# Attention stacks kept by feature in DRAM and read in 4 KB pieces, with another order of work where the second layer begins

## The reference, cut to what matters

```
def rope(t):                       # t1, t2: the two halves of a head's 32 features
    return concat([t1 * cos - t2 * sin, t2 * cos + t1 * sin])
def attn(q, k, v):
    return softmax(q k^T / sqrt(32)) v, heads side by side
xn = adaln(x, cond, ln1);  q, k, v = xn @ qkv_w.T;        x = x + attn(rope(q), rope(k), v) @ sa_out_w.T
xn = adaln(x, cond, ln2);  q = xn @ q_w.T;  k, v = ctx @ k_w.T, ctx @ v_w.T
                                                          x = x + attn(rope(q), rope(k), v) @ ca_out_w.T
xn = adaln(x, cond, ln3);                                 x = x + gelu(xn @ ffn_w1.T + b1) @ ffn_w2.T + b2
```

## Time and profile before

| | |
|---|---|
| median of 3 runs | 1928.59 us (1923.56 to 1931.18) |
| the profiled execution | 1925.28 us, span 1923.5 us |
| mean granted clock of TensorE | 0.994 |
| packets, all queues | 306451, 308.37 MB |
| attention stage | to about 1240 us |

### The profile page before, as it was taken

One profiled execution on the slowest core, in us unless ns is written; L12 is line 12 of the kernel. 1 busy time (PEld: TensorE's weight loads), 2 busy tenths in 40 slices (PEclk: granted clock), 3 DMA queues, 4 the chain that ended last, 5 costly groups with the idle time before them and its releaser, 6 DMA issues. The chain is left out here.

```text
span 1923.5 us, 39339 instructions
## 1 busy us (share of the span) xinstructions
PE 1869.4 (97%) x13460; PEld 1630.4 (85%) x13460; DVE 1294.9 (67%) x2250; ACT 1383.3 (72%) x3813; POOL 785.8 (41%) x818
## 2 busy tenths in 40 slices
PE   8899999999998999999999998899999999999999
PEld 7788888888877888888888886688898998989898
DVE  7766676767776677676776776446667666666754
ACT  4777777888876888888888888655666666565654
POOL 3534433443442454454454441013536354444531
PEclk9999999999998999999999999999999999999999
DMA  7666676566576778767668677343232322323130
GB/s 232 195 203 185 204 223 194 177 200 198 165 220 189 204 212 233 201 197 227 199 200 225 198 217 190 109 137 110 78 99 67 99 88 89 95 71 110 45 99 33
DMA packets 306451, 308.37 MB, mean 160 GB/s; under 512 B 21072, under 2 KB 260048, under 8 KB 306256
## 3 DMA queue, kind: packets, MB, share of 16 engines
q1 hardware_dynamic: 304528, 304.47, 53.4%
q10 hardware_dynamic: 1728, 1.39, 0.3%
HBM read 212.46 MB, written 92.27 MB: 158 GB/s over the span
## 5 line engine op out<-in xcount | busy, mean ns | idle before, releaser
L744 ACT ACTIVATE ps_s<-ps_s,neg_max 128x256 f32<-128x256 f32 x1024 | 452.8, 443 | 55.4 <-DVE neg_max L861 48.3
L861 DVE TENSOR_REDUCE neg_max<-ps_s 128x2 f32<-128x512 f32 x512 | 349.3, 687 | 212.8 <-PE ps_s L615 212.4
L758 ACT ACTIVATE prob<-ps_s 128x512 f32<-128x512 f32 x512 | 303.4, 593 | 137.2 <-PE ps_s L634 134.3
L634 PE MATMUL ps_s<-qT,kT 98*128 98x256 f32 x1024 | 211.6, 289 | 24.4 <-DMA qT<-max_rows 21.8
L931 POOL TENSOR_TENSOR rope_c<-rope_c,rope_s 128x256 f32<-128x256 f32 x128 | 98.4, 769 | 330.5 <-DVE rope_s L836 330.5
L615 PE MATMUL ps_s<-kT,qT 96*128 96x256 f32 x1024 | 216.5, 293 | 10.7 <-ACT ps_s L744 8.3
L615 PEld LDWEIGHTS ps_s<-kT,qT 96*128 96x128 f32 x1024 | 169.9, 190 | 60.3 <-ACT ps_s L744 28.4
L605 PE MATMUL ps_g<-xx_hi,w_hi 128*128 128x256 f32 x1024 | 208.1, 285 | 1.4 <-issue 1.4
L634 PEld LDWEIGHTS ps_s<-qT,kT 98*128 98x128 f32 x1024 | 169.3, 191 | 46.9 <-issue 21.0
L744 ACT ACTIVATION_READ_ACCUMULATOR ps_s<-ps_s,neg_max 128x1 f32 x1024 | 207.8, 203 | 0.0
L605 PE MATMUL ps_g<-xx_lo,w_hi 128*128 128x256 f32 x1024 | 205.5, 282 | 0.0
(11 more groups left out here) (155 smaller groups left out, 4654.7 us busy)
## 6 DMA issues: line engine op xcount, KB each, us to landing
kT<-k_turned SPq DMA_DIRECT2D x384, 128.0 KB, 3.1
qT<-q_turned SPq DMA_DIRECT2D x128, 256.0 KB, 3.9
f_raw<-in_w1T SPq DMA_DIRECT2D x124, 256.0 KB, 3.1
k_turned<-rot_hi SPq DMA_DIRECT2D x64, 256.0 KB, 3.2
k_turned<-rot_lo SPq DMA_DIRECT2D x64, 256.0 KB, 2.5
q_turned<-rot_hi SPq DMA_DIRECT2D x64, 256.0 KB, 3.6
q_turned<-rot_lo SPq DMA_DIRECT2D x64, 256.0 KB, 4.1
qT<-q_turned SPq DMA_DIRECT2D x128, 128.0 KB, 3.9
```

Of the source, the lines that this page charges most:

```text
L634: ins = eng.matmul(ps_s[:, score_bank(step), t * L:(t + 1) * L], kT[:, quad % NQ, j, t * P:(t + 1) * P], qT[:, quad % NQ, j, :], start=Tru ...
L744: ins = eng.activation(scores[:, t * L:(t + 1) * L], scores[:, t * L:(t + 1) * L], ACT.Exp, bias=neg_max[G % 2][:, t, j:j + 1], accum_out= ...
L758: eng.activation(prob[:, n % NP, :, :].rearrange("p t l -> p (t l)"), ps_s[:, score_bank(step), :], ACT.Exp).then_inc(exp_done, 1)
L861: eng.tensor_reduce(neg_max[G % 2][:, :, j], ps_s[:, score_bank(step), :].rearrange("p (t l) -> p t l", l=L), AX.X, ALU.max, negate=True). ...
```

## The change

`turned[m]` gets the shape (2, 2, HD, H, L): item parity, part, feature of a head, head, token, so that one feature of four neighbouring heads is one piece of 4 KB. A spill is made in four copies instead of two (per part and half of the heads' features). A stack is read with two copies for k and two for q: q's rows are high, low, high and k's high, high, low in blocks of 32, and k's two blocks of high come in one copy whose source is repeated. In `stage_order` the places around items 14 to 17 are changed: the projections k, q, v of item 16 and the output projections of item 13 follow each other without a gap, the second layer's weight rows for k, q and v are loaded from place 632 to 707 and split from 668 to 723, and item 17's norm, context and projections come up to six places later.

```diff
--- before.py
+++ after.py
@@ -90,20 +90,20 @@
                 put(p + place, kind, n, h)
         if ahead < N + 2:
 
-            late = 0
+            late = 6 if ahead == B + 1 else 0
             steps = {2: (2, 4, 5, 8, 10), B + 1: (-3, 0, 1, 5, 8), N: (-14, -12, -11, -6, -4),
                      N + 1: (-26, -24, -23, -18, -16)}.get(ahead, (-13, -5, -4, 1, 5))
             for place, step in zip(steps, (("stats", ahead, 0), ("stats", ahead, 1), ("norm", ahead), ("scale", ahead, 0), ("scale", ahead, 1))):
                 put(p + late + place, *step)
-            x_place = p + late + (31 if ahead == B else {N: 6, N + 1: -10}.get(ahead, 22 if ahead == 2 else 18 if B < ahead else 16))
+            x_place = p + late + (29 if ahead == B else {N: 6, N + 1: -10}.get(ahead, 22 if ahead == 2 else 18 if B < ahead else 16))
             for half in range(2):
                 put(x_place + 3 * half, "turn_x", ahead, half)
                 put(x_place + 2 + 3 * half, "x_high", ahead, half)
                 put(x_place + 4 + 3 * half, "x_low", ahead, half)
         if ahead < N:
             if ahead >= B:
-                put(p - 10, "ctx_load", ahead)
-                put(p + 9, "ctx_split", ahead)
+                put(p + (-6 if ahead <= B + 1 else -10), "ctx_load", ahead)
+                put(p + (14 if ahead == B + 1 else 9), "ctx_split", ahead)
             k, q, v = (project(m, ahead, 0) + project(m, ahead, 1) for m in "kqv")
             if ahead in (1, 2):
                 begins = {1: (48, 65, 79), 2: (40, 51, 66)}[ahead]
@@ -119,15 +119,20 @@
                 turns(spread(p + 35, 18, q))
                 spread(p + 68, 16, v)
             else:
-                turns(spread(p + 18, 11, k))
-                spread(*((p + 42, 9, v) if ahead == B else (p + 42, 13, v)))
-            if 2 < ahead < N - 1:
-                turns(spread(*((p + 42, 13, q) if ahead < B else (p + 50, 10, q) if ahead == B else (p + 29, 13, q))))
+                for m, units in zip("kqv", (k, q, v)):
+                    place, count = {B: {"k": (29, 11), "q": (40, 11), "v": (51, 10)},
+                                    B + 1: {"k": (24, 10), "q": (34, 11), "v": (45, 10)}}.get(
+                                        ahead, {"k": (18, 11), "q": (29, 13), "v": (42, 13)})[m]
+                    last = spread(p + place, count, units)
+                    if m != "v":
+                        turns(last)
+            if 2 < ahead < B:
+                turns(spread(p + 42, 13, q))
         if i >= 1:
             put(p + 37, "res_load", i - 1)
 
-            spread(p + (3 if i == N - 1 else 7) + 48, 14 if i >= N - 2 else 9, [("project", "o", i - 1, t, c) for cs in (range(KC - 1), (KC - 1,)) for t in range(T) for c in cs])
-            put(p + 66, "store", i - 1)
+            spread(p + {B - 2: 61, N - 1: 51}.get(i, 55), 14 if i >= N - 2 else 10 if i in (B - 2, B - 1) else 9, [("project", "o", i - 1, t, c) for cs in (range(KC - 1), (KC - 1,)) for t in range(T) for c in cs])
+            put(p + (72 if i == B - 2 else 66), "store", i - 1)
         if i == N - 1:
             put(p + 68, "res_load", i)
             for c in range(KC - 1):
@@ -140,9 +145,11 @@
             weight_rows(44, layer_rows(0, "o"), 4, 8)
             put(60, "b1_load")
         if i == B - 2:
-            weight_rows(p + 6, layer_rows(1, "k"), 3, 8)
-            weight_rows(p + 19, layer_rows(1, "q"), 3, 8)
-            weight_rows(p + 28, layer_rows(1, "v"), 3, 8)
+            for n, m in enumerate("kqv"):
+                for c, row in enumerate(layer_rows(1, m)):
+                    put(p + (-40, 3, 20)[n] + (7, 5, 5)[n] * c, "w_load", *row)
+                    put(p + (-4, 14, 31)[n] + (4, 5, 5)[n] * c, "w_high", *row)
+                    put(p + (-4, 14, 31)[n] + (4, 5, 5)[n] * c + LOW, "w_low", *row)
         if i == B:
             weight_rows(p + 66, layer_rows(1, "o"), 3, 8)
         if i == N - 2:
@@ -325,7 +332,7 @@
     with ExitStack() as whole:
 
 
-        turned = {m: nc.dram_tensor(f"{m}_turned", (2, D, 2, L), F32, kind="Internal").ap() for m in "qk"}
+        turned = {m: nc.dram_tensor(f"{m}_turned", (2, 2, HD, H, L), F32, kind="Internal").ap() for m in "qk"}
 
         def sem(name):
             return whole.enter_context(nc.semaphore(name))
@@ -420,7 +427,7 @@
             stack_in = {m: [sem(f"stack_{m}{n}") for n in range(4)] for m in "qk"}
             max_rows_in = [sem(f"max_rows_in{n}") for n in range(2)]
 
-            STACKS = {"q": 2, "k": 3}
+            STACKS = {"q": 2, "k": 2}
 
             mod_done, mod_turned, x_turned, product_done, scores_done, max_turned, weigh_done, mix_done, rows_used = (
                 sem(n) for n in ("mod_done", "mod_turned", "x_turned", "product_done", "scores_done",
@@ -530,7 +537,7 @@
             def rot_free(n):
 
                 m, i, t = list(ropes)[n - 1 - NT]
-                return spilled[m][t], 32 * (i + 1)
+                return spilled[m][t], 64 * (i + 1)
 
             def attention_tensor(eng):
                 for step in order:
@@ -989,31 +996,32 @@
                         if i >= 2:
                             for quad in (2 * t, 2 * t + 1):
                                 eng.wait_ge(stack_in[m][quad], 16 * STACKS[m] * (i - 1))
-                        out_to = turned[m][i % 2, T * t * P:T * (t + 1) * P].rearrange("(p d) s l -> s p d l", d=2)
+                        heads = slice(t * HG, (t + 1) * HG)
                         eng.wait_ge(rot_hi_done, n)
-                        eng.dma_start(out_to[0], rot_hi[:, n % NT, :, :].bitcast(F32)).then_inc(spilled[m][t], 16)
+                        for half in range(2):
+                            into = turned[m][i % 2, 0, half * HALF:(half + 1) * HALF, heads, :].rearrange("d h l -> h d l")
+                            eng.dma_start(into, rot_hi[:, n % NT, half, :].bitcast(F32)).then_inc(spilled[m][t], 16)
                         eng.wait_ge(rot_lo_done, n)
-                        eng.dma_start(out_to[1], rot_lo[:, n % NT, :, :].bitcast(F32)).then_inc(spilled[m][t], 16)
+                        for half in range(2):
+                            into = turned[m][i % 2, 1, half * HALF:(half + 1) * HALF, heads, :].rearrange("d h l -> h d l")
+                            eng.dma_start(into, rot_lo[:, n % NT, half, :].bitcast(F32)).then_inc(spilled[m][t], 16)
                     elif kind == "b1_load":
                         eng.dma_start(b1_sb[:, :], b1).then_inc(b1_in, 16)
                     elif kind == "stack":
                         m, quad = step[1:]
                         i, n = divmod(quad, 4)
-                        eng.wait_ge(spilled[m][n // 2], 32 * (i + 1))
+                        eng.wait_ge(spilled[m][n // 2], 64 * (i + 1))
                         if quad >= NQ:
                             eng.wait_ge(weigh_done, OH * (quad - NQ + 1))
-                        heads = turned[m][i % 2][n * OH * HD:(n + 1) * OH * HD]
+                        high, low = (turned[m][i % 2, part, :, n * OH:(n + 1) * OH, :].rearrange("d j l -> d (j l)") for part in range(2))
+                        into = (qT if m == "q" else kT)[:, quad % NQ, :, :].rearrange("p h l -> p (h l)").bitcast(F32)
                         if m == "q":
-                            eng.dma_start(qT[0:2 * HD, quad % NQ, :, :].bitcast(F32),
-                                          heads.rearrange("(h d) s l -> (d s) h l", d=HD)).then_inc(stack_in[m][n], 16)
-                            eng.dma_start(qT[2 * HD:ROWS, quad % NQ, :, :].bitcast(F32),
-                                          heads[:, 0].rearrange("(h d) l -> d h l", d=HD)).then_inc(stack_in[m][n], 16)
+                            both = turned[m][i % 2, :, :, n * OH:(n + 1) * OH, :].rearrange("s d j l -> (s d) (j l)")
+                            eng.dma_start(into[0:2 * HD, :], both).then_inc(stack_in[m][n], 16)
+                            eng.dma_start(into[2 * HD:ROWS, :], high).then_inc(stack_in[m][n], 16)
                         else:
-                            for s in range(2):
-                                eng.dma_start(kT[s:2 * HD:2, quad % NQ, :, :].bitcast(F32),
-                                              heads[:, 0].rearrange("(h d) l -> d h l", d=HD)).then_inc(stack_in[m][n], 16)
-                            eng.dma_start(kT[2 * HD:ROWS, quad % NQ, :, :].bitcast(F32),
-                                          heads[:, 1].rearrange("(h d) l -> d h l", d=HD)).then_inc(stack_in[m][n], 16)
+                            eng.dma_start(into[0:2 * HD, :], high.unsqueeze(0).broadcast_to([2, HD, OH * L])).then_inc(stack_in[m][n], 16)
+                            eng.dma_start(into[2 * HD:ROWS, :], low).then_inc(stack_in[m][n], 16)
                     elif kind == "res_load":
                         i = step[1]
                         layer, b = divmod(i, B)
```

## The result

| | median | runs | profiled span | granted clock |
|---|---|---|---|---|
| before | 1927.61 us | 4 | 1923.5 us | 0.994 |
| after | 2336.47 us (2330.70 to 2336.79) | 4 | 2328.9 us | 0.930 |

The ratio is 1.2112, 95% interval 1.2086 to 1.2137: 21% slower. The forecast was 2261, in the range 2040 to 2530.

What follows compares the result with a forecast made beforehand. TensorE bounds the kernel before; after, two DMA engines were to bound the attention stage: 32 x (46.1 - 36.8) = 298 us, +28 for weight rows, +10 for stalls, so 1925.3 + 336 = 2261 us, range 2040 to 2530.

Steps and rivals of the forecast that it cites:

- How the copies are spread: Attention stage's DMA copies: the smaller outermost size decides, so doubled k copy on 2 engines, each spill on 8.
- the open point: Doubled k copy: assumed, unproven, that its repeated source counts like a two-row target, giving 2 engines; other end 16.
- The price of 4 KB: DMA packets of the stacks: 172 ns per 4 KB packet, kept between 144 and 184.
- Two DMA engines become the bound of the stage: Attention stage: engines 0 and 1 need 45.1 to 47.1 us per item where TensorE needs 36.8; +298 us.
- 10 us in all: Attention stage: added for stalls, as rot_hi waits for an earlier spill and ScalarE, SP and later stacks wait behind.
- My last rival: Attention stage: spills queue behind doubled copies, ropes and ScalarE wait; 2357 us at 3 us more per item; chance 0.22.
- the forecast's own sign: Attention stage, if right: TensorE waits for kT<-k_turned, a wait that appeared nowhere before.
- TensorE's clock stays: Attention stage: TensorE keeps full clock at 80% busy, as it was granted 1.00 at 19.78 of 24 us.
- The boundary: 10 us, if TensorE stays the bound: Change of layer: new places leave no stretch without projections; 0 to 15 us saved, 10 taken.
- SP's extra issues at nothing: SP's queue: +2.0 us of issues per item, 16.4 becoming 18.4 of 36.8 us, hidden by slack.
- The rival on the other side: Attention stage: copies spread over all 16 engines, queues a little lighter, TensorE stays the bound; 1910 us, chance 0.12.
- 28 us were added for weight rows: Weight loads: some 40 single weight rows, 0.7 us each, no longer hidden, +28 us.

Runs made afterwards that it cites:

- the first experiment: The changed kernel with k's repeated high part read as (feature, copy) instead of (copy, feature), so its copy runs on 16 engines: 1990.98 us, ratio 1.0312.
- the wide kernel: The changed kernel with every copy on 16 engines and q, k weight columns reordered at layout: 1935.16 us with two copies per spill, 1943.07 us with four.

## Why the prediction was right, and where not

- **How the copies are spread: right.** 2 engines for the doubled copy and 8 for a spill follow from the count of small packets, 3840 fewer. That a repeated source counts like a short target was the open point, and the first experiment shows it. The rule of the Trainium skill (DMA: Bandwidth & Descriptors, Rules for kernel authors) on a leading zero-stride broadcast holds here: 345 of 409 us. That narrow copies use the same engines follows from their neighbours: the maximum rows' copy, itself on 2 engines, took 6.7 us at the median of 64, and 3.3 with the doubled copies spread; had the doubled copies rotated over the engines, most of the 64 would have met free ones. Which two they are, no trace here tells.
- **The price of 4 KB: a little high.** 164 ns for 172.
- **"Two DMA engines become the bound of the stage": right for the second layer, too little for the first.** It gave 46.1 us per item; the 64 copies of maximum rows give 49.1 (from 79.8 to 1627.9 us). In the second layer a steady item takes 46.6 us and the queues never run empty. In the first it takes 54.4, with less load (no context), and in 5.4% of the time no engine has a packet: so there more than the load sets the pace. What fits are the late landings, of the maximum rows for TensorE and of the spills for ScalarE, for which the forecast had 10 us in all. Even the load is not a sum at fixed prices: 6 us less of it bought 0.8, and equal loads gave 2160, 2220 and 2257 us. My last rival (stalls pile up, 2357 at 3 us per item above the bound) describes the case better. Its sign came too, ScalarE waiting for a landing (126.7 us); the forecast's own sign, TensorE waiting for kT<-k_turned, did not, q's stack and the maximum rows being the last to land.
- **"TensorE's clock stays": wrong.** Busy share 80% was right (1268 of the 1570 us from 80 to 1650), but there were waits of up to 7.9 us, and the granted clock was 0.81 to 0.95 in windows of 48 us. The row that I took (19.78 of 24 us at full clock) was a stretch with shorter waits, up to 1.7 us. TensorE's matmuls took 129 us more; how much of the 405 us that made is not shown.
- **The boundary: 10 us, if TensorE stays the bound: wrong.** It is 0 (1.0003). More projections in the gap took 2.3 us from the waits for exponentials and brought 2.8 us of new waits, for low parts that VectorE had not written yet. What it overlooked beside that: the largest wait, 7.0 us for the maximum rows, has its own path (at 573.53 and 601.52 us before, ScalarE issued the copy, and TensorE went on 3.4 and 3.6 us later), which does not get shorter by more projections around it. The timeline before also has 2.19 us of waiting for exponentials at 600.25, which the prediction did not name.
- **SP's extra issues at nothing: slightly wrong.** 8 us in the wide kernel, where spills and their counting packets doubled and the DRAM layout changed with them. In the change itself it can't be told apart.
- **The rival on the other side, 1910 us: wrong even on its own condition.** With all copies wide it is 1935; longer pieces do not make the queues lighter.

The forecast of 2261 lies 75 us below the measured time. The mechanism was the right one, but part of the closeness is luck: the first layer's lateness, 8 us per item above the forecast's pace, was left out, while 32 items were counted at the full price though the last two pay none, and 28 us were added for weight rows that no run shows by themselves.

**What stays open:** how the 15 us that an item of the first layer takes more divide between load and lateness, and why 6 us less load bought under 2 us per item in the second layer too (46.6 to 45.0). The runs show both at work and that the place of the narrow copy moves the wait, but no run holds one fixed while the other goes to nothing. No version tried beats the kernel before.

## What to carry to other kernels

Count the small packets of a window with one copy in it: they say on how many DMA engines it runs. In these runs the smaller of the two sides' outermost sizes decided (2, 8, or 16 for sizes of 16, 32, 64 and 128), a repeated dimension included. Put a repeat inside and such a size outside. A narrow copy costs more than its own time, since every copy on 16 engines has a share on its engines; look for it at its neighbours, in waits for small copies that were harmless before.

## What was not expected of the hardware

- Pieces of 4 KB are no cheaper per byte than pieces of 1 KB in this traffic: 52.9% against 53.4% of 16 engines' span for the same bytes, though 76 thousand packets were saved.
- The same two-row copy on 2 engines with 8 packets each is not slower than on 8 engines in two copies, which take a second issue: 21.8 us of waits against 37.0.
- A lower busy share of the DMA engines (43.6% for 53.4%) can go with later landings: 12.4 us for 3.3 at the median of the 16 stores shown.
